# Regrouping the routed slots, shortening the store lag and moving the row weighting to ScalarE in an AdaLN mixture-of-experts block

## The chip, the core and the metric

One core of a Trainium2 chip runs the whole kernel. The metric is the device time of one execution in microseconds; of the kernel before, three runs are known, with a median of 580.17 us (579.09 to 580.22).

## What is computed

The input x holds 32 sequences of 256 rows of 128 float32 values: 8192 rows. Per sequence, six vectors come from a small product (`mod = silu(c) @ wmod`). Then:

```
h = layernorm(x) * (1 + ca) + sa
x = x + ga * attention(h)          # linear attention, 32 memory channels
h = layernorm(x) * (1 + cb) + sb
gate = softmax(h @ w_gate.T); the two best of 8 experts per row, with their scores
x = x + gb * sum over the two of  score * (gelu(h @ W1[e] + b1[e]) @ W2[e] + b2[e])
```

The hidden width of an expert is 512. Only the two chosen experts of a row are computed.

## The kernel before, in words

**Attention steps.** Two sequences make a pair (4 tiles of 128 rows), 16 pairs in all. A software pipeline of steps (`steps`, L231) runs on PE, DVE and ACT; step p handles the projections of pair p, the attention product of pair p-1 and the second norm and the logits of pair p-2. Steps -1 to 3 and 14 to 17 are written out, the ones between run in loops of two steps each. Eight steps also turn one piece of the expert weights into float16 high and low parts (`weights_high` L519 on ACT, `weights_low` L736 on DVE), and SP moves each piece back (`move`, L365), behind the load of a memory matrix and the clearing of a part of the slot buffer (L382 to L388).

**Routing.** The pairs form three groups (`GPAIRS`, L23). After a group's pairs, `route` (PE L1100, ACT L617, DVE L827) picks two experts per row and gives each row two places (`POS`) in a DRAM buffer of slots: a slot is 256 rows of one expert. A group of n tiles has n + 7 slots (`ST`, L33), so the three groups have 31, 31 and 23, in all 85. POOL then scatters the rows with indirect DMAs (`scatter`, L473), two per tile: 128 DMAs in all.

**Slots.** After all steps a loop of 85 slots runs in ten turns of 8 and a rest (`ffn_loop`, L249). For slot t PE does `up(t)` and then `down(t-2)` (L1112, L1123), ACT the Gelu of t (L627), DVE the high and low split of t-1 and the result rows of t-3 (L942, L951). SP's queue (`ring`, L357) alternates: the load of slot t, which waits until `up(t-4)` is done, and then the store of slot t - LAG, which waits for that slot's rows. LAG is 8.

**Gathering and mixing.** The results return to the rows in 16 chunks of 4 tiles. POOL's queue holds first all scatters; then for each group it waits until all slots of the group are stored and gathers the group's chunks, 8 indirect DMAs per chunk (`gather`, L483, the DMA is L490), and after each chunk's DMAs it waits for the chunk before and flags it (`landed`, L494, the memset L497). The ring has 8 places, so the gather of chunk c waits until chunk c-8 is mixed. DVE mixes a chunk in four passes (`mix`, L960): both results by their scores (L967), their sum (L971), by the gate (L976), onto x (L979). Chunks 0 to 3 are mixed in turns 6 to 9 of the slot loop, one pass after every second slot (`MIX0`, L49, is 31 // 8 + 3 = 6), chunks 4 to 15 after the loop (L983). SP writes a mixed chunk out (L411), 16 in all, after all stores.

Of the kernel before, what the change touches and what calls it, by code (L numbers as in the profile page):

```python
# [6 lines left out]
def build_adaln_block(nc, A):  # L7
    f32, f16 = mybir.dt.float32, mybir.dt.float16
    i32, u32 = mybir.dt.int32, mybir.dt.uint32
    ALU, ACT, AX = mybir.AluOpType, mybir.ActivationFunctionType, mybir.AxisListType  # L10
    ds = bass.ds

    BATCH, SEQ, D = 32, 256, 128
# [4 lines left out]
    PAIRS = BATCH // 2  # L18
# [1 line left out]
    W = D + 1  # L20
    LN_EPS, CLIP = 1e-5, 1e-6

    GPAIRS = (6, 6, 4)  # L23
    GROUPS = len(GPAIRS)
    PAIRS_TO = [sum(GPAIRS[:g + 1]) for g in range(GROUPS)]
    GT = tuple(n * PT for n in GPAIRS)
# [6 lines left out]
    ST = tuple(2 * TOK * n // SLOT + E - 1 for n in GT)  # L33
    S0 = tuple(sum(ST[:g]) for g in range(GROUPS + 1))
    SLOTS = S0[-1]
    LAG = 2 * RING
    BODY = 2 * RING
    TURNS = SLOTS // BODY
    JT = 2 * TOK * GTM // 2 // SLOT
# [6 lines left out]
    LOOPED = 4  # L46
    ZS = 8
    ZERO0 = tuple(sum(-(-s // ZS) for s in ST[:g]) for g in range(GROUPS + 1))
    MIX0 = S0[1] // BODY + 3  # L49
    KB = FF // 128  # L50

    ctx = ExitStack()
    with ctx:
# [6 lines left out]
        def sem(name):  # L60
            return ctx.enter_context(nc.semaphore(name))
# [145 lines left out]
        y_out = [sem(f"y_out{k}") for k in range(RING)]  # L207
        up_done, g_ready = sem("up_done"), sem("g_ready")
        ghigh_ready, glow_ready, down_done, y_ready = sem("ghigh_ready"), sem("glow_ready"), sem("down_done"), sem("y_ready")
        gathered = [sem(f"gathered{n}") for n in range(2)]  # L210
        rows_in, mix_link, mixed, out_done = sem("rows_in"), sem("mix_link"), sem("mixed"), sem("out_done")

        block = ctx.enter_context(nc.Block())
# [1 line left out]
        def ge(eng, s, v):  # L215

            if isinstance(v, int) and v <= 0:
                return
            eng.wait_ge(s, v)
# [11 lines left out]
        def steps(eng, step, route, after={}, weights=False, last=lambda: None):  # L231


            for p in range(-1, 4):
                step(p, p % 2, p // 2)
                after.get(p, lambda: None)()

            for first, end, n_of, g in ((0, 2, 0, 0), (2, 4, 1, None), (4, 5, None, 1)):
                with eng.Fori(first, end) as n:
                    for k in range(2):  # L240
                        step(2 * n + 4 + k, k, n + 2, **({"weights": n_of} if weights and n_of is not None else {}))
                if g is not None:
                    route(g)
            for p in range(PAIRS - 2, PAIRS + 2):
                step(p, p % 2, p // 2)
            last()
            route(GROUPS - 1)

# [61 lines left out]
        def _(sp):  # L310
# [46 lines left out]
            def ring(n, g=None, h=None):  # L357

                for k in range(RING):
                    if not isinstance(n, int) or RING * n + k < SLOTS:  # L360
                        load(g, n, k)
                    if not isinstance(n, int) or LAG <= RING * n + k < SLOTS + LAG:
                        store(h, n - LAG // RING, k)

            def move(c):  # L365

# [15 lines left out]
            for p in range(LOOPED, PAIRS):  # L382
                sp.wait_ge(fold_ready, p - EARLY + 1)
                if p > LOOPED + 1:
                    sp.wait_ge(mem_done, p - 1)
                sp.dma_start(MR[:, p % 2, :], MEMO[:, p, :]).then_inc(mr_in[p % 2], 16)
                clear(p - LOOPED)
                move(2 * (p - LOOPED - 1))  # L388

            for i in range(2):  # L390
                sp.wait_ge(ws_moved[i], 16 * (E + 1))
# [2 lines left out]
            sp.dma_start(GA[:].rearrange("p (b d) -> p b d", d=D),  # L394
                         gsc[:, D:2 * D].rearrange("(o b) d -> o b d", o=1).broadcast_to([128, BATCH, D])).then_inc(gb_in, 16)
            ring(1)
            n = LAG // RING
            cuts = sorted(S0[1:] + tuple(s + LAG for s in S0[1:-1]))
            for cut in cuts:
                if cut // RING - n > 1:  # L400
# [112 lines left out]
        def _(act):  # L513
# [28 lines left out]
            def step(p, j, half, weights=None):  # L542
                q, r = p - 1, p - 2
                if has(r):

                    ge(act, var_ready, r + 1)
                    nc.scalar.activation(rstd2[:, 1, :], rstd2[:, 0, :], ACT.Ln).then_inc(ln2_ln, 1)
                    ge(act, ln2_ln, r + 1)
                    nc.scalar.activation(rstd2[:, 2, :], rstd2[:, 1, :], ACT.Exp, scale=-0.5).then_inc(ln2_exp, 1)
                if has(p - 3):  # L550
                    rows(p - 3)
                if has(p):

                    ge(act, qk_done, p + 1)
                    ge(act, sig_ready, p)
                    nc.scalar.activation(RL[:], psQK[:, 0:SEQ], ACT.Relu, scale=-1.0).then_inc(rl_link, 1)
                    ge(act, rl_link, p + 1)
                    nc.scalar.activation(EX[:], RL[:], ACT.Exp, scale=-1.0).then_inc(er_ready, 1)
                if has(q):

                    ge(act, am_ready, q + 1)
                    nc.scalar.activation(AM[:, :, TOK:SEQ], psS.rearrange("p (b c) -> p b c", b=2)[:, :, TOK:SEQ],
                                         ACT.Copy).then_inc(am_side, 1)
                if has(r):

                    ge(act, xn2_turned, r + 1)
                    ge(act, lo_ready, r)
                    if isinstance(r, int) and r == 0:
                        act.wait_ge(bnd_all, 2)
                    for b in range(2):  # L570
                        last = nc.scalar.activation(  # L571
                            H2T[:, b * SEQ:(b + 1) * SEQ], psH[:, b * SEQ:(b + 1) * SEQ], ACT.Identity,
                            bias=modT[:, ds(3 * BATCH + 2 * r + b, 1)], scale=modT[:, ds(4 * BATCH + 2 * r + b, 1)])
                    last.then_inc(h2t_ready, 1)
                    ge(act, h2t_ready, r + 1)
                    ge(act, parts_turned, r)
                    nc.scalar.activation(HH[:], H2T[:], ACT.Copy).then_inc(hi_ready, 1)  # L577
                if has(p + 1):

                    if isinstance(p, int) and p + 1 in NORMS:  # L580
                        act.wait_ge(ln1_ready, NORMS.index(p + 1) + 1)
                    ge(act, xn_turned, p)
                    for t in range(PT):
                        last = nc.scalar.activation(XN[:, 1 - j, t * D:(t + 1) * D], X[:, ds((p + 1) * PT * D + t * D, D)],  # L584
                                                    ACT.Identity, bias=shift1[:, ds((p + 1) * PT + t, 1)],
                                                    scale=rstd1[:, ds((p + 1) * PT + t, 1)])
                    last.then_inc(xn_ready, 1)
                if has(p):

                    ge(act, sig_ready, p + 1)  # L590
                    for b in range(2):
                        last = nc.scalar.activation(KT[b * 64:b * 64 + DM, j, :], SIG[b * 64 + DM:b * 64 + 64, j, :],
                                                    ACT.Copy)
                    last.then_inc(kt_ready, 1)
                if weights is not None:
                    act.wait_ge(ws_ready, 4)
                    weights_high(2 * half - 4 + j, weights)
                if has(p):
                    ge(act, v_done, p + 1)
                    ge(act, av_done, p - 1)  # L600
                    if isinstance(p, int) and p == 0:
                        act.wait_ge(const_ready, 4)
                    nc.scalar.activation(VP[:, j, :, 1:W], psV[:].rearrange("p (t d) -> p t d", d=D),
                                         ACT.Copy).then_inc(vp_ready, 1)
                if has(p + 1):

                    if isinstance(p, int) and p == -1:
                        act.wait_ge(mod_ready, 1)
                    ge(act, xn_turned, p + 2)
                    ge(act, v_done, p)  # L610
                    for b in range(2):
                        last = nc.scalar.activation(
                            HT[:, 1 - j, b * SEQ:(b + 1) * SEQ], psX[:, b * SEQ:(b + 1) * SEQ], ACT.Identity,
                            bias=modT[:, ds(2 * (p + 1) + b, 1)], scale=modT[:, ds(BATCH + 2 * (p + 1) + b, 1)])
                    last.then_inc(hT_ready, 1)
# [20 lines left out]

            act.wait_ge(pos_ready, 1)
            ffn_loop(act, ((0, gelu, True),))

        TOP, TINY = 2.0 ** 14, 2.0 ** -40  # L640

# [5 lines left out]
        def _(dve):  # L647
# [96 lines left out]
            def step(p, j, half, weights=None):  # L744
# [75 lines left out]
                    nc.vector.tensor_scalar(LGT[:, ds(r * PT * E, PT * E)], psQK[:, SEQ:SEQ + PT * E], x_scales[:, 4:5], None,  # L820
                                            ALU.mult).then_inc(lgt_ready, 1)
                if weights is not None:
                    weights_low(4 * half - 8 + 2 * j, weights)

            route_link = links(dve, route_step, 0)

# [130 lines left out]
                nc.vector.scalar_tensor_tensor(out=halves(YR[:, k, :]), in0=halves(psD[k % 2][:, 0:SH * D]),  # L957
                                               scalar=f_scales[:, 4:5], in1=bias, op0=ALU.mult, op1=ALU.add).then_inc(y_ready, 1)

            def mix(c, place, part):  # L960

                y = YG[:, ds(place * 2 * CH * D, 2 * CH * D)].rearrange("p (k t d) -> p k t d", k=2, t=CH)
                if part == 0:
# [2 lines left out]
                    cw = CW[:, :, ds(c * CH, CH)].rearrange("p k (t o) -> p k t o", o=1).broadcast_to([128, 2, CH, D])  # L966
                    nc.vector.tensor_tensor(y, y, cw, ALU.mult).then_inc(mix_link, 1)  # L967
                    return
                ge(dve, mix_link, 3 * c + part)
                if part == 1:  # L970
                    nc.vector.tensor_tensor(y[:, 0], y[:, 0], y[:, 1], ALU.add).then_inc(mix_link, 1)  # L971
                elif part == 2:
# [7 lines left out]

            dve.wait_ge(pos_ready, GROUPS)
            ffn_loop(dve, ((-1, split, False), (-3, rows, True)), mix)
            for first, last in ((TURNS - MIX0, YRING), (YRING, CHUNKS)):  # L983
                with dve.Fori(first, last) as c:
                    for part in range(4):
                        mix(c, c - first // YRING * YRING, part)

        @block.tensor
        def _(pe):
# [181 lines left out]
```

## Time and profile before

| | us |
|---|---|
| median of 3 runs | 580.17 |
| the profiled execution's own time | 579.69 |
| its span | 578.0 |
| DVE busy | 464.3 (80%) |
| PE busy | 379.8 (66%) |
| POOL busy | 314.8 (54%) |
| ACT busy | 305.3 (53%) |

The page gives, of one profiled execution, the busy time of each engine, the span in 40 slices of 14.45 us, and the chain of work that ended last. The timeline gives single instructions: its first number is the start in us from the start of the span, its second the duration in us. "SPq" is SP's queue of DMA issues. A busy time of POOL at an indirect DMA is the time in which it prepares the transfer, not the transfer.

### The profile page before, as it was taken

Reading aid. Unit: us, or ns where it says so; the run is one execution under the profiler, and the core shown is the slowest. Engines: PE = TensorE matmul, PEld = TensorE weight load, DVE = VectorE, ACT = ScalarE, POOL = GpSimd, SP = SyncE. Lnnn points to the kernel's source line nnn. Section 1 sums busy time; section 2 is a strip of 40 time slices with the busy share of each in tenths; the row PEclk is TensorE's granted clock in tenths of the full one; section 3 lists DMA queues with packets and bytes.
Section 4 is the critical chain, followed back from the end, with each engine's and each line's share of the span. In section 5 each row is a group of like instructions: output and inputs, shape, how many; then the busy total and the mean of one; then the engine's idle time right before and its main releaser. Section 6 shows DMA issues by size and latency. Waiting matters only on the chain.

```text
span 578.0 us, 14761 instructions
## 1 busy us (share of the span) xinstructions
PE 379.8 (66%) x4184; PEld 337.1 (58%) x4185; DVE 464.3 (80%) x1092; ACT 305.3 (53%) x658; POOL 314.8 (54%) x344
## 2 busy tenths in 40 slices
PE   3550557761877718428999999999999999700000
PEld 3350546650766617317989999998989889600000
DVE  4669888888888898666888888899999999786424
ACT  1441557981898817417667776677666666400000
POOL 3258100001777727777777200778860887788672
PEclk9955777875788958758999999999999999955555
DMA  3499002543558522513755443556553555453231
GB/s 107 146 344 341 2 1 65 154 140 92 157 164 237 168 51 87 166 50 91 143 142 145 109 100 93 143 141 136 139 127 93 131 132 138 114 161 112 64 86 54
DMA packets 129664, 73.19 MB, mean 127 GB/s; under 512 B 53728, under 2 KB 122976, under 8 KB 129376
## 3 DMA queue, kind: packets, MB, share of 16 engines
q1 hardware_dynamic: 121440, 56.02, 35.0%
q0 software_dynamic: 8192, 16.79, 11.0%
q8 instruction: 14, 0.23, 0.2%
q14 instruction: 18, 0.15, 0.1%
HBM read 21.75 MB, written 34.90 MB: 98 GB/s over the span
## 4 chain that ended last, share of the span: by engine, by line
PE 38%; DVE 26%; POOL 16%; issue 10%; ACT 4%; DMA 3%; DVEq 2%; SPq 0%; ACTq 0%; POOLq 0%
PE psA L1131 16%; POOL ROW L490 16%; PE psA L1119 8%; PE psV L1119 4%; PE psH L1119 4%; DVE ATT L734 3%; PE psH L1029 2%; DVE X L803 2%; DMA X<-in_x 2%; DVE stats L677 2%; DVE stats L810 2%; DVE w_bound L913 2%; ACT HH L577 1%; ACT ATT L571 1%; DVE HL L796 1%
## 5 line engine op out<-in xcount | busy, mean ns | idle before, releaser
L490 POOL DMA_INDIRECT ROW<-slot_out,POS x128 | 150.0, 1172 | 93.5 <-DMA slot_out<-VP 54.6
L479 POOL DMA_INDIRECT slot_rows<-ROW,POS x128 | 131.5, 1027 | 115.1 <-DVE EXPT L888 76.7
L1131 PE MATMUL psA<-WST,ATT 128*128 x2040 | 139.0, 221 | 2.1 <-DVE VP L957 1.6
L1131 PEld LDWEIGHTS psA<-WST,ATT 128*128 128x128 f16 x2040 | 124.9, 98 | 12.4 <-issue 3.7
L948 DVE SCALAR_TENSOR_TENSOR ATT<-ATT,f_scales 128x1024 f16<-128x1024 f32 x85 | 109.2, 1284 | 3.0
L632 ACT ACTIVATE ATT<-psA,b1T,f_scales 128x256 f32<-128x256 f32 x172 | 83.1, 564 | 35.7 <-PE psA L1119 35.7
L946 DVE TENSOR_SCALAR ATT<-ATT,f_scales 128x1024 f16<-128x1024 f32 x85 | 65.3, 768 | 21.9 <-ACT ATT L632 21.2
L1119 PE MATMUL psA<-WT,WST 128*128 128x256 f16 x516 | 65.7, 279 | 5.7 <-DVE RT L876 3.7
L632 ACT ACTIVATE ATT<-psV,b1T,f_scales 128x256 f32<-128x256 f32 x84 | 42.9, 561 | 36.9 <-PE psH L1119 35.2
L1119 PEld LDWEIGHTS psA<-WT,WST 128*128 x516 | 48.5, 99 | 13.5 <-issue 6.2
L1029 PE MATMUL psH<-ident,ATT 128*128 128x128 f32 x64 | 14.2, 360 | 57.1 <-DVE ATT L734 57.1
L1029 PEld LDWEIGHTS psH<-ident,ATT 128*128 128x128 f32 x64 | 9.1, 178 | 64.9 <-DVE ATT L734 64.9
L632 ACT ACTIVATE ATT<-psH,b1T,f_scales 128x256 f32<-128x256 f32 x84 | 42.9, 567 | 0.0
L957 DVE SCALAR_TENSOR_TENSOR VP<-psA,f_scales,b2B 128x256 f32<-128x256 f32 x85 | 40.5, 478 | 1.9 <-PE psA L1131 1.9
L967 DVE TENSOR_TENSOR ROW<-ROW,CW x16 | 19.6, 1223 | 25.4 <-POOL flag L497 25.3
L1119 PE MATMUL psV<-WT,WST 128*128 128x256 f16 x252 | 34.7, 275 | 0.0
L1119 PE MATMUL psH<-WT,WST 128*128 128x256 f16 x252 | 34.4, 273 | 0.0
L571 ACT ACTIVATE ATT<-psH,modT 128x256 f32<-128x256 f32 x32 | 16.3, 560 | 27.9 <-PE psH L1029 27.9
L584 ACT ACTIVATE ATT<-X,shift,rstd 128x128 f32<-128x128 f32 (+1 forms) x64 | 26.2, 479 | 0.9 <-DVE shift L687 0.9
L1119 PEld LDWEIGHTS psH<-WT,WST 128*128 x252 | 24.7, 98 | 2.9
L796 DVE TENSOR_TENSOR HL<-ATT,HH 128x512 f16<-128x512 f32 x16 | 11.1, 693 | 17.4 <-ACT HH L577 17.4
L1049 PE MATMUL psV<-GA,ATT 128*128 128x128 f32 (+1 forms) x128 | 25.0, 361 | 0.0
(199 smaller groups left out, 696.4 us busy)
## 6 DMA issues: line engine op xcount, KB each, us to landing
slot_out<-VP SPq DMA_DIRECT2D x85, 128.0 KB
slot_rows<-zero SPq DMA_DIRECT2D x8, 1024.0 KB, 7.2
X<-in_x SPq DMA_DIRECT2D x8, 512.0 KB, 7.4
WST<-in_W SPq DMA_DIRECT2D x2, 2048.0 KB, 11.8
WST<-WT SPq DMA_DIRECT2D x16, 256.0 KB, 2.3
out<-X SPq DMA_DIRECT2D x16, 256.0 KB, 2.4
slot_rows<-zero SPq DMA_DIRECT2D x3, 896.0 KB, 4.8
slot_rows<-ROW,POS POOLq DMA_INDIRECT x128
```

Source lines behind the costliest of these rows:

```text
L479: nc.gpsimd.indirect_dma_start(xg[g], bass.IndirectOffsetOnAxis(ap=POS[:, k * TILES + t:k * TILES + t + 1], axis=0), ROW[:, t * 2 * D:(t + ...
L490: nc.gpsimd.indirect_dma_start(YG[:, o:o + D], None, yg[g], bass.IndirectOffsetOnAxis(ap=POS[:, i:i + 1], axis=0)).then_inc(gathered[c % 2 ...
L571: last = nc.scalar.activation(H2T[:, b * SEQ:(b + 1) * SEQ], psH[:, b * SEQ:(b + 1) * SEQ], ACT.Identity, bias=modT[:, ds(3 * BATCH + 2 * ...
L584: last = nc.scalar.activation(XN[:, 1 - j, t * D:(t + 1) * D], X[:, ds((p + 1) * PT * D + t * D, D)], ACT.Identity, bias=shift1[:, ds((p + ...
L632: last = nc.scalar.activation(G[:, k % 2, m * SLOT:(m + 1) * SLOT], psU[k % 2][m // 2][:, m % 2 * SLOT:(m % 2 + 1) * SLOT], ACT.Gelu, bias ...
L946: nc.vector.tensor_scalar(GH[:, k % 2, :], G[:, k % 2, :], f_scales[:, 3:4], None, ALU.mult).then_inc(ghigh_ready, 1)
L948: nc.vector.scalar_tensor_tensor(out=GL[:, k % 2, :], in0=G[:, k % 2, :], scalar=f_scales[:, 3:4], in1=GH[:, k % 2, :], op0=ALU.mult, op1= ...
L957: nc.vector.scalar_tensor_tensor(out=halves(YR[:, k, :]), in0=halves(psD[k % 2][:, 0:SH * D]), scalar=f_scales[:, 4:5], in1=bias, op0=ALU. ...
L1029: last = nc.tensor.transpose(psH[:, t * D:(t + 1) * D], XN2[:, t * D:(t + 1) * D], ident[:])
L1049: last = mm(psV[:, t * D:(t + 1) * D], HT[:, j, t * TOK:(t + 1) * TOK], GA[:, ds((2 * p + t // 2) * D, D)], start=True, stop=True)
L1119: last = mm(o, W1S[:, ds(e * 2 * FF + a * FF + m * 128, 128)], XT[:, k, b * SLOT:(b + 1) * SLOT], start=(c == 0), stop=(c == 2))
L1131: last = mm(psD[k % 2][:, h * D:(h + 1) * D], a[:, k % 2, i:i + TOK], W2S[:, ds(e * 2 * FF + b * FF + m * D, D)], start=(m == 0 and c == 0 ...
```

## The change

Four things. The groups become 7, 5 and 4 pairs: 28, 20 and 16 tiles, with 35, 27 and 23 slots, still 85; `steps` and SP's moves are rearranged to it (the eight weight pieces go to steps 5 to 12 instead of 4 to 11; the first routing follows step 8 instead of 7, the second follows step 13 as before). LAG becomes 6. `MIX0` is written with + 2; 35 // 8 + 2 is 6. After its last Gelu, ACT multiplies the gathered rows of chunks 4 to 14 by their scores, one instruction of 128x128 for each of 8 tiles, and DVE does three passes for these chunks instead of four; chunk 15 keeps four passes on DVE.

```diff
-    GPAIRS = (6, 6, 4)
+    GPAIRS = (7, 5, 4)
...
-    LAG = 2 * RING
+    LAG = 6
...
-    MIX0 = S0[1] // BODY + 3
+    MIX0 = S0[1] // BODY + 2
+    MIXED = TURNS - MIX0
...
-            for p in range(-1, 4):
+            for p in range(-1, 5):
                 step(p, p % 2, p // 2)
                 after.get(p, lambda: None)()
 
-            for first, end, n_of, g in ((0, 2, 0, 0), (2, 4, 1, None), (4, 5, None, 1)):
+            for g, (first, end) in enumerate(((2, 4), (4, 6))):
                 with eng.Fori(first, end) as n:
                     for k in range(2):
-                        step(2 * n + 4 + k, k, n + 2, **({"weights": n_of} if weights and n_of is not None else {}))
-                if g is not None:
+                        step(2 * n + 1 + k, 1 - k, n + k, **({"weights": (g, 2 * n - 4 + k)} if weights else {}))
+                if g == 0:
                     route(g)
-            for p in range(PAIRS - 2, PAIRS + 2):
+            for p in range(PAIRS - 3, PAIRS + 2):
                 step(p, p % 2, p // 2)
+                if p == PAIRS_TO[1] + 1:
+                    route(1)
...
-                        store(h, n - LAG // RING, k)
+                        store(h, n + (k - LAG) // RING, (k - LAG) % RING)
...
-                move(2 * (p - LOOPED - 1))
+                move(2 * (p - LOOPED - 2))
...
             ffn_loop(act, ((0, gelu, True),))
+
+            act.wait_ge(pos_ready, GROUPS)
+            for first, last in ((MIXED, YRING), (YRING, CHUNKS - 1)):
+                with act.Fori(first, last) as c:
+                    ge(act, rows_in, c + 1)
+                    for k in range(2):
+                        for t in range(CH):
+                            y = YG[:, ds((c - first // YRING * YRING) * 2 * CH * D + (k * CH + t) * D, D)]
+                            done = nc.scalar.activation(y, y, ACT.Copy, scale=CW[:, k, ds(c * CH + t, 1)])
+                    done.then_inc(scaled, 1)
...
-                ge(dve, mix_link, 3 * c + part)
+                if part == 1 and by_act:
+                    ge(dve, scaled, c - MIXED + 1)
+                else:
+                    ge(dve, mix_link, (3 * c if base is None else base) + part)
...
-            for first, last in ((TURNS - MIX0, YRING), (YRING, CHUNKS)):
+            for first, last in ((MIXED, YRING), (YRING, CHUNKS - 1)):
                 with dve.Fori(first, last) as c:
-                    for part in range(4):
-                        mix(c, c - first // YRING * YRING, part)
+                    for part in range(1, 4):
+                        mix(c, c - first // YRING * YRING, part, 3 * MIXED + 2 * (c - MIXED) - 1, True)
+            for part in range(4):
+                mix(CHUNKS - 1, CHUNKS - 1 - YRING, part, 3 * MIXED + 2 * (CHUNKS - 1 - MIXED))
```

## Rows read from the trace of the kernel before

**Rows 1.** The page, part 2: busy tenths of PE and POOL in 40 slices
```profile
PE   3550557761877718428999999999999999700000
...
POOL 3258100001777727777777200778860887788672
```

**Rows 2.** The page, part 4: the chain that ended last, by line
```profile
PE psA L1131 16%; POOL ROW L490 16%; PE psA L1119 8%; PE psV L1119 4%; PE psH L1119 4%; DVE ATT L734 3%; PE psH L1029 2%; DVE X L803 2%; DMA X<-in_x 2%; DVE stats L677 2%; DVE stats L810 2%; DVE w_bound L913 2%; ACT HH L577 1%; ACT ATT L571 1%; DVE HL L796 1%
```

**Rows 3.** Timeline of POOL: start us, us, line, out<-in, count, idle before and releaser
```profile
142.00 1.31 POOL L479 DMA_INDIRECT slot_rows<-ROW,POS  x1 [66.33 <-DVE EXPT L888]
...
359.98 0.99 POOL L490 DMA_INDIRECT ROW<-slot_out,POS  x1 [37.74 <-DMA slot_out<-VP]
...
429.95 0.09 POOL L497 MEMSET flag<- 1x1 f32 x1
446.92 2.09 POOL L490 DMA_INDIRECT ROW<-slot_out,POS  x1 [16.88 <-DMA slot_out<-VP]
...
506.17 0.09 POOL L497 MEMSET flag<- 1x1 f32 x1
...
510.30 1.44 POOL L490 DMA_INDIRECT ROW<-slot_out,POS  x1 [0.30 <-issue]
512.04 1.77 POOL L490 DMA_INDIRECT ROW<-slot_out,POS  x1 [0.30 <-issue]
...
521.71 1.42 POOL L490 DMA_INDIRECT ROW<-slot_out,POS  x1 [0.22 <-issue]
...
534.79 0.95 POOL L490 DMA_INDIRECT ROW<-slot_out,POS  x1 [0.21 <-issue]
...
567.09 0.09 POOL L497 MEMSET flag<- 1x1 f32 x1
```

**Rows 4.** Timeline of SP's queue in the slots
```profile
357.00 0.58 SPq L355 DMA_DIRECT2D slot_out<-VP  x1
...
361.43 1.20 SPq L347 DMA_TRANSPOSE WT<-slot_rows  x1
...
437.37 1.19 SPq L347 DMA_TRANSPOSE WT<-slot_rows  x1
...
440.02 1.19 SPq L347 DMA_TRANSPOSE WT<-slot_rows  x1
...
444.12 0.58 SPq L355 DMA_DIRECT2D slot_out<-VP  x1
```

**Rows 5.** Timeline of DVE at slot 61's rows and at the last slot's
```profile
438.47 0.48 DVE L957 SCALAR_TENSOR_TENSOR VP<-psA,f_scales,b2B 128x256 f32<-128x256 f32 x1
...
503.61 0.48 DVE L957 SCALAR_TENSOR_TENSOR VP<-psA,f_scales,b2B 128x256 f32<-128x256 f32 x1 [1.89 <-PE psA L1131]
```

**Rows 6.** Timeline of DVE after the slots: passes of the first chunk and the last
```profile
504.13 1.23 DVE L967 TENSOR_TENSOR ROW<-ROW,CW  x1
505.50 0.69 DVE L971 TENSOR_TENSOR ROW<-ROW  x1
...
507.24 0.69 DVE L979 TENSOR_TENSOR X<-X,ROW  x1
...
574.35 0.69 DVE L979 TENSOR_TENSOR X<-X,ROW  x1
```

**Rows 7.** Timeline of ACT in one attention step and at the last slot
```profile
167.34 1.64 ACT L584 ACTIVATE ATT<-X,shift,rstd 128x128 f32 x4
...
496.90 1.93 ACT L632 ACTIVATE ATT<-psA,b1T,f_scales 128x256 f32<-128x256 f32 x4 [0.73 <-PE psA L1119]
```

**Rows 8.** Timeline of SP's queue in the attention steps
```profile
117.15 1.13 SPq L370 DMA_DIRECT2D WST<-WT  x2
...
127.90 1.13 SPq L370 DMA_DIRECT2D WST<-WT  x2
...
205.07 5.68 SPq L347 DMA_TRANSPOSE WT<-slot_rows  x4
```

**Rows 9.** Timeline of PE at the first slot
```profile
257.82 2.74 PE L1119 MATMUL psA<-WT,WST 128*128 128x256 f16 x12 [3.71 <-DVE RT L876]
```

More of the change, by code:

```diff
@@ L209, in build_adaln_block @@
         ghigh_ready, glow_ready, down_done, y_ready = sem("ghigh_ready"), sem("glow_ready"), sem("down_done"), sem("y_ready")
-        gathered = [sem(f"gathered{n}") for n in range(2)]
+        gathered, scaled = [sem(f"gathered{n}") for n in range(2)], sem("scaled")
         rows_in, mix_link, mixed, out_done = sem("rows_in"), sem("mix_link"), sem("mixed"), sem("out_done")
@@ L396, in _ @@
             ring(1)
-            n = LAG // RING
+            n = 2
             cuts = sorted(S0[1:] + tuple(s + LAG for s in S0[1:-1]))
@@ L596, in step @@
                     act.wait_ge(ws_ready, 4)
-                    weights_high(2 * half - 4 + j, weights)
+                    weights_high(weights[1], weights[0])
                 if has(p):
@@ L822, in step @@
                 if weights is not None:
-                    weights_low(4 * half - 8 + 2 * j, weights)
+                    weights_low(2 * weights[1], weights[0])
             route_link = links(dve, route_step, 0)
@@ L958, in rows, with mix @@
                                                scalar=f_scales[:, 4:5], in1=bias, op0=ALU.mult, op1=ALU.add).then_inc(y_ready, 1)
-            def mix(c, place, part):
+            def mix(c, place, part, base=None, by_act=False):
                 y = YG[:, ds(place * 2 * CH * D, 2 * CH * D)].rearrange("p (k t d) -> p k t d", k=2, t=CH)
```

## The prediction, made blind

> **What bounds the kernel now.** First the slices of the page, then the chain, then POOL's timeline. The slices [rows 1] show three stretches: attention, the slots at nine tenths of PE from slice 18 to slice 34, and an end in which PE does nothing and POOL works. The chain that ended last [rows 2] gives 16% of the span, 92 us, to the gathers of L490. That is more than the end after the slots (503.6 to 578), so the chain leaves PE while the slots still run. POOL's timeline [rows 3] shows where. Its gathers of group 0 run from 359.98 to 429.95: 48 in 70.0 us. It then sits idle for 16.9 us until slot 61's store has landed, and from 446.92 it never again waits for another engine: chunks 6 to 10 until the flag at 506.17, chunk 11 until 521.71, chunks 12 to 15 until the flag at 567.09. The last slot's rows are finished at 503.61 + 0.48 = 504.09 [rows 5]. So group 2's gathers could start at about 507 and start at 521.71, because POOL is one chunk behind. The end is set by POOL's backlog, and behind it by two mixes and the last write.
>
> **Regrouping: one chunk leaves the stretch after slot 61.** Group 1 now has 5 chunks instead of 6; the slots, scatters and gathers keep their number. Where does group 0's seventh chunk go? Group 0 is stored with slot 34 instead of 30. Slot 30's store is issued at 357.00 [rows 4] and the gather follows at 359.98 [rows 3], 2.98 later. With LAG 6 the store of slot 34 stands behind the load of slot 40, which is two loads after load 38 and starts at 361.43 [rows 4]; 1.2 for the load's own issue gives 362.6, and the first gather at 365.6, 5.6 later than now. Its first 48 gathers then end at about 429.95 + 5.6 = 435.6, and eight more at 1.33 (70.0 us / 48 is 1.46, with longer gathers in it that come once a turn; I take 10.9 for this chunk) end at 446.5. That is the moment at which group 1 starts today (446.92), so POOL's 16.9 us of idle time take up the chunk. Chunks 7 to 11 then take what chunks 6 to 10 take now, 506.17 - 446.92 = 59.3, and POOL is free at 506.
>
> **LAG 6.** Slot 61's store is issued at 444.12, behind load 69; it now follows load 67 of 437.37 and the rows of slot 61, ready at 438.47 + 0.48 = 438.95 [rows 4, 5]. It is 5.2 earlier, lands at about 441, and is off the path, as POOL is still on group 0. What counts is slot 34's store: at LAG 8 it would be 5.5 later and the whole chain of gathers with it. Behind the waiting store stands the next load, 68: it can't go before 440.02 today, since it waits for PE [rows 4], and the store's issue of 0.4 to 0.6 from 438.95 is over by then. So no load moves. The cover is half a microsecond wide, and a rival below is about it. At the end of the slots nothing changes, since no load stands before the last stores.
>
> **Steps, routing and scatters.** The number of steps, of steps with weights (8), of clears (12 instead of 11, one piece more but the same order of bytes) and of routings stays. SP's order of memory load, clear and move is only shifted by one step, as are the pieces it waits for, so no memory load stands behind another wait than before. The first routing comes one step later, 127.90 - 117.15 = 10.75 [rows 8], so POOL's scatters start at 142.00 + 10.75 = 152.8 instead of 142.00 [rows 3]. The first 56 at 1.27 end at 224, and slot 0's loads, now at 205.07 [rows 8], come at about 226, still 32 us ahead of PE's first slot at 257.82, which waits for the last routing [rows 9]. All scatters end at 322 now (359.98 - 37.74, rows 3), at most 10.75 later then, and still before 365.6. The wider routing tiles (28 tiles instead of 24 in the first, 20 in the second) cancel. I put all of this at 0; for what the trace can't show (a step that meets scatters at another moment) I bound it by 1 us either way. MIX0 remains 6, so this edit does nothing; its first rows are flagged about 5.6 later, at 387, and used from turn 6 on, at 399, so DVE doesn't wait.
>
> **The gathers of group 2.** Their start is the later of POOL (506), the last store and chunk 4's mix. The last store can be issued at 504.1; from slot 61's store to the gather it took 446.92 - 444.12 = 2.8 [rows 3, 4], which makes 507.0. ACT ends its last Gelu at 496.90 + 1.93 = 498.8 [rows 7] and needs, by the four 128x128 instructions in 1.64 [rows 7], 0.41 each, 8 x 0.41 = 3.3 per chunk, 3.4 with the loop. Chunk 4 is weighted at 502.3, DVE's three passes take 507.93 - 505.50 = 2.4 [rows 6] and end at 506.6. So 507.0, where it is 521.71 now: 14.7 gained.
>
> How fast are they? While DVE mixes without a break, two gathers with their gaps take 1.44 + 0.30 + 1.77 + 0.30 = 3.8, 1.9 each [rows 3]. Once DVE waits, 24 gathers take 567.09 - 534.79 = 32.3, 1.35 each. In the rows the long gathers end together with one of DVE's passes of 0.69. After the change the seven chunks 4 to 10, which have been gathered, come to DVE every 3.4 us from ACT, and chunk 11 follows: DVE mixes until about 529. In such a period a gather that is held to the end of a pass fits twice: 1.7 each, against bounds of 1.35 (no hold) and 1.9 (as now). I take 1.7: 13 gathers until 529.1. The other 19 at 1.35 take 25.6, and the last flag but one comes at 554.7 instead of 567.09: 12.4 gained of the 14.7.
>
> The Trainium skill (SBUF — State Buffer, Who interferes with whom) would have it otherwise: a VectorE tensor_tensor with two inputs in SBUF contends with GpSimd's reads, and, as it infers, not with the writing of descriptors. By it all 32 gathers would go at 1.35. The trace of before does not agree: they go at 1.9 beside these passes [rows 3, 6].
>
> **The end.** Today, from the flag at 567.09: 0.36, four passes for chunk 14, four for chunk 15 (3.8 each), and from 574.35 + 0.69 = 575.04 to 578.0 the last write, 10.9 in all [rows 3, 6]. Now ACT's 3.4 and three passes (2.5) stand for chunk 14's 3.8: 2.1 more, 13.0. DVE can't use the wait for chunk 15, since it stands behind it in its queue. The span ends at 554.7 + 13.0 = 567.7, 10.3 less. The weighting instruction is not in the trace; L584 has its shape and engine and is my lower bound. The upper one is the Gelu of 128x256 at 1.93 / 4 = 0.48 [rows 7]: then this end is 0.6 longer, and the stretch of mixing 8 x 0.56 = 4.5 longer, with 2.6 gathers more at 1.7 instead of 1.35, 0.9: 1.5 us in all, which the range holds.
>
> **The sum.** 579.69 - 10.3 = 569.4 on the profiled execution, which lies 0.5 under the median; against the median it is 569.9. I say 569.7.
>
> **Rivals.**
> (a) The gathers of group 2 run undisturbed, since DVE has gaps (also what the page's rule gives by itself): 32 x 1.35 = 43.2 from 507.0, flag at 550.2, end at 563.2, time 565. For it speak the fast gathers beside single chunks; against it the locked pairs of today. Chance 0.17.
> (b) POOL arrives late or stays slow: its spare time before 507.0 is one microsecond by my sum, so a first gather two slots later (5.5), slower gathers in the slots, or ACT at 0.48 give 572 to 576 (569.7 + 5.5 = 575.2 for the first). Chance 0.18.
> (c) Slower: the store's wait holds up the loads. Place: SP's queue, load t+7 behind store t. Today load 68 leaves half a microsecond for it; in turns with a mix pass DVE's rows can be later by that pass (0.69). If PE then waited for its input in each of 79 slots, 10.3 / 79 = 0.13 us per slot would eat the gain, and 0.5 us per slot would give 579.7 - 10.3 + 40 = 609. Against it: the input of a slot is loaded three slots ahead, 8 us. Chance 0.04.
> (d) No change: the backlog isn't what counts, as the gathers are limited by their transfers and the group's total of 128 is the same. Against it: POOL's busy time with its fixed gaps of 0.30 fills that stretch. Chance 0.03.
>
> The forecast itself, 567 to 572, has 0.58. The range leaves out the far side of (b), (c) and (d): 564.5 to 574.5. About 0.2% (1.2 us) can be told from no change here: faster 0.93, same 0.03, slower 0.04.
>
> **What would show it.** Gathers in one run without a wait for stores between group 0 and group 1; the first gather near 365.6; a gap of at most a few us before group 2, whose first gather starts near 507; gathers of 1.7 with gaps until about 529; ACT at 3.4 per chunk; 13 us from the last flag but one to the end; PE's slots ending at 503.5 as now. Wrong it would be if PE's slots ended later (rival c), if group 2 started after 510 (rival b), or if the end after the flag were over 15 us.

## The result and the profile after

The changed kernel takes 571.18 us (median of four runs, 571.0 to 572.52), the kernel before 580.19 in the same comparison. The ratio is 0.9841, 95% interval 0.9822 to 0.9860: 9.0 us less by the medians, 9.2 by the ratio. Forecast were 569.7 us, with a range of 564.5 to 574.5. The profiled execution after is the longest of the four: it took 572.52, with a span of 570.8.

The first view is again the page, its busy slices and its chain by line. L493 is the gather, L1137 and L1149 are the slots' matmuls.

```profile
PE   3551646874377646626999999999999999930000
...
POOL 2248200000277777777777500077878878788671
...
PE psA L1149 16%; POOL ROW L493 14%; PE psA L1137 8%; PE psV L1137 4%; PE psH L1137 4%; DVE ATT L747 3%; PE psH L1047 3%; DVE X L816 2%; DMA X<-in_x 2%; DVE stats L690 2%; DVE stats L823 2%; DVE w_bound L926 2%; ACT HH L580 1%; ACT ATT L574 1%; DVE AM L778 1%
```

Against [rows 1], POOL's empty slices lie together between scatters and gathers, and the dents (2 among the scatters, 0 among the gathers) are gone. The gathers' share of the chain fell from 16% to 14% [rows 2]. POOL's timeline shows the same in single rows:

```profile
371.50 1.06 POOL L493 DMA_INDIRECT ROW<-slot_out,POS  x1 [47.87 <-DMA slot_out<-VP]
...
454.18 1.35 POOL L493 DMA_INDIRECT ROW<-slot_out,POS  x1 [0.30 <-issue]
455.52 0.09 POOL L500 MEMSET flag<- 1x1 f32 x1
455.83 1.02 POOL L493 DMA_INDIRECT ROW<-slot_out,POS  x1 [0.23 <-DMA slot_out<-VP]
...
513.17 0.09 POOL L500 MEMSET flag<- 1x1 f32 x1
513.48 1.44 POOL L493 DMA_INDIRECT ROW<-slot_out,POS  x1 [0.22 <-issue]
515.23 1.23 POOL L493 DMA_INDIRECT ROW<-slot_out,POS  x1 [0.30 <-issue]
516.76 1.13 POOL L493 DMA_INDIRECT ROW<-slot_out,POS  x1 [0.30 <-issue]
518.19 1.46 POOL L493 DMA_INDIRECT ROW<-slot_out,POS  x1 [0.30 <-issue]
...
536.39 0.94 POOL L493 DMA_INDIRECT ROW<-slot_out,POS  x1 [0.21 <-issue]
539.49 1.14 POOL L493 DMA_INDIRECT ROW<-slot_out,POS  x1 [2.16 <-issue]
...
559.05 0.09 POOL L500 MEMSET flag<- 1x1 f32 x1
```

What to see: between group 0 (from 371.50) and group 1 (from 455.83) there is no idle time, where 16.88 us stood in [rows 3]. But neither is there any before group 2, which starts at 513.48. The last slot's rows are done at 506.44 + 0.48 = 506.92, so POOL is still 3.7 us behind what the stores would allow (506.92 + 2.9, the time from a store to the gather that waited for it). The queue, not the last store, still sets the end.

SP's queue at slot 34 and DVE's and ACT's timelines after the slots:

```profile
366.47 1.19 SPq L350 DMA_TRANSPOSE WT<-slot_rows  x1
368.71 0.37 SPq L358 DMA_DIRECT2D slot_out<-VP  x1
369.12 1.19 SPq L350 DMA_TRANSPOSE WT<-slot_rows  x1
```

```profile
368.20 0.48 DVE L970 SCALAR_TENSOR_TENSOR VP<-psA,f_scales,b2B 128x256 f32<-128x256 f32 x1
...
506.44 0.48 DVE L970 SCALAR_TENSOR_TENSOR VP<-psA,f_scales,b2B 128x256 f32<-128x256 f32 x1 [1.89 <-PE psA L1149]
506.89 0.69 DVE L987 TENSOR_TENSOR ROW<-ROW  x1
507.81 0.69 DVE L992 TENSOR_TENSOR ROW<-ROW,GA  x1 [0.23 <-DVE ROW L987]
508.65 0.69 DVE L995 TENSOR_TENSOR X<-X,ROW  x1
509.30 0.69 DVE L987 TENSOR_TENSOR ROW<-ROW  x1
...
522.87 0.69 DVE L995 TENSOR_TENSOR X<-X,ROW  x1
528.66 0.69 DVE L987 TENSOR_TENSOR ROW<-ROW  x1 [5.10 <-ACT ROW L650]
...
562.09 0.69 DVE L987 TENSOR_TENSOR ROW<-ROW  x1 [8.01 <-ACT ROW L650]
```

```profile
501.54 16.46 ACT L650 ACTIVATE ROW<-ROW,CW  x56
...
559.38 2.44 ACT L650 ACTIVATE ROW<-ROW,CW  x8 [8.01 <-POOL flag L500]
```

In the order of the views: slot 34's store (368.71) leaves 0.03 us after its rows (368.20 + 0.48), and the next load goes right behind it. ACT weighs seven chunks in 16.46, so 2.4 each, and DVE takes a chunk every 2.4 (506.89 to 509.30).

The stretches of two executions can be compared only from a common mark, since the attention part varies (shown below). The table gives, from the first slot's first matmul on: the first gather, the first gather of group 2, the last flag but one, and the end of the span. The marks come from one profile of each kernel, the times are medians; the kernel before was measured anew beside each set of runs (580.2 to 581.2), and the ratio is to that.

| kernel | first gather | group 2 | flag | end | time | ratio to before (95%) |
|---|---|---|---|---|---|---|
| before | 102.2 | 263.9 | 309.3 | 320.2 | 580.2 | 1 |
| changed | 111.3 | 253.2 | 298.8 | 310.6 | 571.2 | 0.9841 (0.9822-0.9860) |
| LAG 8 | 113.5 | 254.8 | 299.9 | 311.7 | 572.8 | 0.9869 (0.9840-0.9897) |
| LAG 7 | 110.7 | 252.6 | 298.2 | 309.9 | 571.4 | 0.9848 (0.9825-0.9872) |
| groups 6, 6, 4 | 99.6 | 257.2 | 301.8 | 313.5 | 574.8 | 0.9892 (0.9855-0.9928) |
| four passes on DVE | 111.0 | 254.4 | 304.0 | 314.9 | 575.6 | 0.9923 (0.9894-0.9952) |
| fewer gathers | 111.1 | 249.5 | 293.6 | 305.3 | 565.9 | 0.9749 (0.9727-0.9771) |
| ACT to chunk 13 | 111.0 | 252.9 | 298.5 | 308.3 | 569.8 | 0.9819 (0.9799-0.9839) |
| before, ACT alone | 101.7 | 260.3 | 303.9 | 315.5 | 576.4 | 0.9929 (0.9902-0.9955) |
| before, LAG 6 alone | 99.8 | 260.0 | 306.5 | 317.4 | 578.8 | 0.9958 (0.9941-0.9975) |

### The profile page after: what moved, and what is told of

It is laid out like the page before. It is cut to its first block, busy times and chain, and to the rows that moved or that the text cites. A ratio compares the mean times of both kernels' runs of the same rounds, so it can differ in the third digit from the quotient of the medians.

```text
span 570.8 us, 14921 instructions
## 1 busy us (share of the span) xinstructions
PE 382.1 (67%) x4184; PEld 339.5 (59%) x4185; DVE 450.4 (79%) x1081; ACT 331.5 (58%) x746; POOL 312.9 (55%) x344
## 3 DMA queue, kind: packets, MB, share of 16 engines
q0 software_dynamic: 8192, 16.79, 11.1%
## 4 chain that ended last, share of the span: by engine, by line
PE 39%; DVE 27%; POOL 14%; issue 10%; ACT 4%; DMA 3%; DVEq 2%; ACTq 0%; SPq 0%
PE psA L1149 16%; POOL ROW L493 14%; PE psA L1137 8%; PE psV L1137 4%; PE psH L1137 4%; DVE ATT L747 3%; PE psH L1047 3%; DVE X L816 2%; DMA X<-in_x 2%; DVE stats L690 2%; DVE stats L823 2%; DVE w_bound L926 2%; ACT HH L580 1%; ACT ATT L574 1%; DVE AM L778 1%
## 5 line engine op out<-in xcount | busy, mean ns | idle before, releaser
L493 POOL DMA_INDIRECT ROW<-slot_out,POS x128 | 147.0, 1148 | 86.6 <-DMA slot_out<-VP 48.1
L1149 PE MATMUL psA<-WST,ATT 128*128 x2040 | 139.1, 221 | 2.0 <-DVE VP L970 1.6
L1149 PEld LDWEIGHTS psA<-WST,ATT 128*128 128x128 f16 x2040 | 125.0, 98 | 12.3 <-issue 3.6
L1137 PE MATMUL psA<-WT,WST 128*128 128x256 f16 x516 | 65.7, 279 | 5.9 <-DVE RT L889 3.7
L1137 PEld LDWEIGHTS psA<-WT,WST 128*128 x516 | 48.4, 99 | 13.9 <-issue 6.6
L650 ACT ACTIVATE ROW<-ROW,CW x88 | 26.2, 395 | 34.0 <-POOL flag L500 34.0
L987 DVE TENSOR_TENSOR ROW<-ROW (+1 forms) x16 | 11.0, 689 | 31.2 <-ACT ROW L650 31.2
L1137 PE MATMUL psV<-WT,WST 128*128 128x256 f16 x252 | 34.8, 275 | 0.0
L1137 PE MATMUL psH<-WT,WST 128*128 128x256 f16 x252 | 34.4, 273 | 0.0
L574 ACT ACTIVATE ATT<-psH,modT 128x256 f32<-128x256 f32 x32 | 16.3, 560 | 28.7 <-PE psH L1047 28.7
L1137 PEld LDWEIGHTS psH<-WT,WST 128*128 x252 | 24.7, 98 | 2.9
L809 DVE TENSOR_TENSOR HL<-ATT,HH 128x512 f16<-128x512 f32 x16 | 11.1, 693 | 18.4 <-ACT HH L580 18.4
```

Of the source, the lines that this page charges most:

```text
L493: nc.gpsimd.indirect_dma_start(YG[:, o:o + D], None, yg[g], bass.IndirectOffsetOnAxis(ap=POS[:, i:i + 1], axis=0)).then_inc(gathered[c % 2 ...
L574: last = nc.scalar.activation(H2T[:, b * SEQ:(b + 1) * SEQ], psH[:, b * SEQ:(b + 1) * SEQ], ACT.Identity, bias=modT[:, ds(3 * BATCH + 2 * ...
L650: done = nc.scalar.activation(y, y, ACT.Copy, scale=CW[:, k, ds(c * CH + t, 1)])
L1137: last = mm(o, W1S[:, ds(e * 2 * FF + a * FF + m * 128, 128)], XT[:, k, b * SLOT:(b + 1) * SLOT], start=(c == 0), stop=(c == 2))
L1149: last = mm(psD[k % 2][:, h * D:(h + 1) * D], a[:, k % 2, i:i + TOK], W2S[:, ds(e * 2 * FF + b * FF + m * D, D)], start=(m == 0 and c == 0 ...
```

## The experiments

**The kernel before, a second profile.** No edit.

> The kernel before, unchanged, for a second profile. In the first profiles the first slot's matmuls start at 257.8 us before and at 260.2 us after the change. Theory A: the change itself costs the attention part 2 us; then this run starts its slots at 257.5 to 258.1. Rival B: the start varies from execution to execution by 1 to 3 us whatever the kernel; then it starts somewhere between 257 and 261, and the slots that follow take 245.8 us as before (from the first matmul to the last slot's rows).

```profile
261.75 2.74 PE L1119 MATMUL psA<-WT,WST 128*128 128x256 f16 x12 [3.71 <-DVE RT L876]
```

The same program starts its slots 3.9 us later than in [rows 9], and took 582.89. From the mark on its span is 319.4 (320.2 before). A falls, and B holds, with a start somewhat beyond its 261: the 2.4 us by which the changed kernel's profile starts its slots later (260.24) are no effect of the change that these profiles could tell. Over all profiles here the first slot starts at 257.4 to 261.7 (median 259.8) in the ten with the changed steps, and at 257.8 to 261.8 (median 259.5) in the four with those of before.

**LAG 8.**

```diff
-    LAG = 6
+    LAG = 2 * RING
```

> The changed kernel with LAG back at 8. Theory A: the gathers form one run from slot 34's store to the end, so every us of that store counts, but at LAG 8 it left SP only 2.2 us after the rows were ready, and at LAG 6 it leaves at once: first gather, first gather of group 2 and the end all 2.2 us later, time 573.4. Rival B (my blind sum): a store two loads earlier is 5.5 us earlier, so LAG 8 costs 5.5: 576.7. Rival C: the last slot's store sets group 2, and the lag costs nothing: 571.2.

572.76 us. First gather 2.2 later, as A has it; of that 1.6 reach group 2 and 1.1 the end. The intervals of the two ratios overlap, so the size rests on the profiles. DVE's rows of slot 34 and SP's queue show why it is not 5.5:

```profile
367.66 0.48 DVE L970 SCALAR_TENSOR_TENSOR VP<-psA,f_scales,b2B 128x256 f32<-128x256 f32 x1
...
369.07 1.19 SPq L350 DMA_TRANSPOSE WT<-slot_rows  x1
370.31 0.58 SPq L358 DMA_DIRECT2D slot_out<-VP  x1
372.03 1.19 SPq L350 DMA_TRANSPOSE WT<-slot_rows  x1
```

At LAG 8 slot 34's store (370.31) goes 1.24 behind the start of its load, and that load starts 0.9 after the rows (367.66 + 0.48).

**Groups of 6, 6 and 4.**

```diff
-    GPAIRS = (7, 5, 4)
+    GPAIRS = (6, 6, 4)
...
-    MIX0 = S0[1] // BODY + 2
+    MIX0 = S0[1] // BODY + 3
...
-                pe.wait_ge(vp_ready, min(PAIRS, PAIRS_TO[g] + 2))
-                pe.wait_ge(row_ready, PAIRS_TO[g])
+                pe.wait_ge(vp_ready, (9, 14, 16)[g])
+                pe.wait_ge(row_ready, (7, 12, 16)[g])
```

> The changed kernel with groups of 6, 6 and 4 pairs again, its steps, lag and ScalarE weighting kept. Theory A: six chunks follow slot 61's store instead of five behind an unbroken queue; first gather of group 1 at about 447, of group 2 at about 520.5 instead of 513.5, some of it given back since fewer gathers meet the mixing: time about 576.5. Rival B (my blind sum): the regrouping is worth a whole chunk and the last store sets group 2's start, 13 us: 584, slower than before the change. Rival C: POOL isn't the limit, 571.2.

574.79 us, 3.6 above the changed kernel, and 2.9 from the mark to the end. Its ratio's interval just touches that of the changed kernel, and the marks agree. The mechanism is A's, its size smaller: 4.0 of A's 7 us at group 2, 3.6 of 5.3 in the time. POOL again waits 16.3 us for slot 61; but the first gather comes 11.7 us earlier (99.6 against 111.3), so the regrouping is worth 16.3 - 11.7 = 4.6 at most, and 4.0 arrive at group 2.

**Four passes on DVE.** ACT's loop is taken out, and DVE's last loops are those of the kernel before.

```diff
-            act.wait_ge(pos_ready, GROUPS)
-            for first, last in ((MIXED, YRING), (YRING, CHUNKS - 1)):
...
-            for first, last in ((MIXED, YRING), (YRING, CHUNKS - 1)):
+            for first, last in ((MIXED, YRING), (YRING, CHUNKS)):
                 with dve.Fori(first, last) as c:
-                    for part in range(1, 4):
-                        mix(c, c - first // YRING * YRING, part, 3 * MIXED + 2 * (c - MIXED) - 1, True)
-            for part in range(4):
-                mix(CHUNKS - 1, CHUNKS - 1 - YRING, part, 3 * MIXED + 2 * (CHUNKS - 1 - MIXED))
+                    for part in range(4):
+                        mix(c, c - first // YRING * YRING, part)
```

> The changed kernel with all four passes of chunks 4 to 15 on VectorE again. Theory A: VectorE's unbroken passes hold up POOL's gathers; seven chunks in 26.7 us let 14 gathers through at 1.9 us each, where three passes per chunk let 19 through in the same time, which costs 5 x 1.28 = 6.4 us; the end after the last flag but one is 0.9 us shorter (10.9 instead of 11.75): time 576.7. Rival B (tensor_tensor passes don't hold up the gathers' descriptors): only the end changes, 570.3. Rival C: the weighting moves nothing but the end, and the gathers' rate of the first chunks is set by the stores' and outputs' traffic: 570.3 with gathers of 1.5 us as now.

575.57 us, 4.4 more, where A said 5.5. POOL's timeline at group 2's first gathers, to be set beside the same rows of the changed kernel above:

```profile
513.35 1.76 POOL L493 DMA_INDIRECT ROW<-slot_out,POS  x1 [0.23 <-issue]
515.42 1.44 POOL L493 DMA_INDIRECT ROW<-slot_out,POS  x1 [0.30 <-issue]
517.16 1.76 POOL L493 DMA_INDIRECT ROW<-slot_out,POS  x1 [0.31 <-issue]
519.23 1.44 POOL L493 DMA_INDIRECT ROW<-slot_out,POS  x1 [0.30 <-issue]
```

Pairs of 3.8 are back, where three gathers take 513.48 to 518.19 = 4.7 in the changed kernel: 1.9 against 1.57. The 32 gathers of group 2 take 49.7 instead of 45.6, chunk 11 before them meets the same (group 2 starts 1.1 later), and the end is 0.9 shorter. B and C fall. The page of the Trainium skill that infers that tensor_tensor passes leave the writing of descriptors alone (SBUF — State Buffer, Who interferes with whom) does not agree with this pair of runs, as far as it is meant for indirect DMAs: what differs there is one VectorE pass in four, done by ScalarE instead, and the gathers beside the passes take 1.9 or 1.57. But the same section of the Trainium skill also states that such passes contend with GpSimd instructions that read SBUF, and each of these gathers takes its row numbers (`POS`) from there. The runs don't show which of the two holds them up.

**Fewer gathers.** Chunks 0 to 11 gather 6 of their 8 pieces; the output lacks two tiles of the second expert's results in each.

```diff
-                    for t in range(CH):
+                    for t in range(CH if k == 0 or c >= 12 else CH - 2):
...
-                pool.wait_ge(gathered[c % 2], 16 * 2 * CH * (c // 2 + 1))
+                pool.wait_ge(gathered[c % 2], 16 * (6 * min(c // 2 + 1, 6) + 8 * max(c // 2 - 5, 0)))
```

> The changed kernel, in which chunks 0 to 11 gather only 6 of their 8 pieces (two tiles of the second expert's results are left out of the output), so that POOL reaches group 2 some 34 us before the last slot is stored. Theory A: then the last store sets group 2's start, 2.9 us after the last slot's rows, 3.6 us earlier than now against the first slot; about three more gathers meet the mixing and give 0.8 back: time 568.4. Rival B: POOL's queue isn't what holds group 2 back: 571.2. The slots themselves keep their 246 us under either.

565.91 us, 5.3 less, where A said 2.8. POOL's timeline, and in it the last store and the end of chunk 4's mix:

```profile
485.15 1.21 POOL L493 DMA_INDIRECT ROW<-slot_out,POS  x1 [4.14 <-DVE X L995]
...
493.01 0.65 POOL L500 MEMSET flag<- 1x1 f32 x1
...
503.75 0.37 SPq L358 DMA_DIRECT2D slot_out<-VP  x1
505.44 0.69 DVE L995 TENSOR_TENSOR X<-X,ROW  x1
...
506.93 0.94 POOL L493 DMA_INDIRECT ROW<-slot_out,POS  x1 [13.27 <-DVE X L995]
...
540.85 0.94 POOL L493 DMA_INDIRECT ROW<-slot_out,POS  x1 [0.21 <-issue]
542.09 0.94 POOL L493 DMA_INDIRECT ROW<-slot_out,POS  x1 [0.30 <-issue]
...
551.01 0.09 POOL L500 MEMSET flag<- 1x1 f32 x1
```

Group 2 starts at 506.93 - 257.42 = 249.5 from the mark, 3.7 earlier: A holds for the start, and the floor is reached. The row names chunk 4's mix as what came last (DVE's L995 at 505.44 + 0.69 = 506.13), but that was done 0.8 us before. Chunk 11's first gather (485.15), which waited for such a pass, came 0.3 after it (484.20 + 0.68 = 484.88). The last store was issued 3.2 before the gather, about what other stores took to their gathers (2.6 to 3.0), so the store is the likelier one; the profile doesn't settle it. The rest is a thing that I had not counted: the pause of 2.16 us after the first gather of chunk 14, in the timeline above, is missing here (540.85, 542.09).

**ScalarE only to chunk 13.**

```diff
-            for first, last in ((MIXED, YRING), (YRING, CHUNKS - 1)):
+            for first, last in ((MIXED, YRING), (YRING, CHUNKS - 2)):
...
-            for part in range(4):
-                mix(CHUNKS - 1, CHUNKS - 1 - YRING, part, 3 * MIXED + 2 * (CHUNKS - 1 - MIXED))
+            for c in (CHUNKS - 2, CHUNKS - 1):
+                base = 3 * MIXED + 2 * (CHUNKS - 2 - MIXED) + 3 * (c - CHUNKS + 2)
+                for part in range(4):
+                    mix(c, c - YRING, part, base)
```

> The changed kernel with chunk 14 weighted by VectorE too (ScalarE does chunks 4 to 13). Theory A: after the last flag but one VectorE's first sum starts 3.0 us later now (ScalarE's 2.44 and its wake-up); with its own pass of 1.23 it starts after 0.4 + 1.4 = 1.8, so the end is 1.2 us earlier: 570.0. Rival B: the last chunk's own landing (1.6 us after that flag) or its store bounds the end: 571.2.

569.84 us, 1.3 less, where A said 1.2; the intervals of the two ratios overlap. DVE and POOL at the end:

```profile
558.29 0.09 POOL L500 MEMSET flag<- 1x1 f32 x1
558.48 1.22 DVE L980 TENSOR_TENSOR ROW<-ROW,CW 128x1024 f32<-128x1024 f32 x1 [5.16 <-POOL flag L500]
559.74 0.69 DVE L987 TENSOR_TENSOR ROW<-ROW 128x512 f32<-128x512 f32 x1
```

The sum of chunk 14 starts 1.45 after the flag, against 562.09 - 559.05 = 3.04 in the changed kernel. These passes are written out, which also takes away the small gaps between them that the loop has.

**ScalarE for chunk 15, VectorE for chunk 14.** As the last one, with ACT's eight instructions for chunk 15 behind its loop and three passes on DVE.

```diff
+            act.wait_ge(rows_in, CHUNKS)
...
+            dve.wait_ge(scaled, CHUNKS - 1 - MIXED)
+            for part in range(1, 4):
+                mix(CHUNKS - 1, CHUNKS - 1 - YRING, part, base + 2)
```

> The changed kernel with VectorE weighting chunk 14 and ScalarE chunk 15. Theory A: after the last flag but one VectorE is through chunk 14 at 0.4 + 3.6 = 4.0 us, ScalarE through weighting chunk 15 at 1.6 + 0.3 + 2.4 = 4.3; then three passes, so the end is 0.9 us shorter than where VectorE weighs both (569.8): 569.0. Rival B: the last write and what is ahead of it in its queue bound the end: 569.8.

569.51 us, ratio 0.9811 (0.9785 to 0.9836), against 0.9819. By the profile the end after the flag is 567.5 - 558.16 = 9.3 instead of 9.8; the times can't tell the two kernels apart. Both lie below the changed kernel, but all three intervals overlap; that either beats it rests on the end measured in the profiles (9.8 and 9.3 us instead of 11.75) and on medians 1.3 and 1.7 lower, and is not shown beyond that.

**LAG 7.**

```diff
-    LAG = 6
+    LAG = 7
```

> The changed kernel with LAG 7. Theory A: the store of slot t stands behind load t+7, which goes when the matmuls of slot t+3 are done, just before the rows of slot t are; so it leaves with the rows as at LAG 6: 571.2, first gather 111.3 us after the first slot's matmul. Rival B: each slot of lag costs the same, half of what LAG 8 costs: 572.0 and 112.4.

571.35 us, first gather at 110.7 from the mark: A, with 0.6 that no theory named and that is within what profiles differ by.

**ACT's weighting alone, on the kernel before.** The same edits as in the change to ACT and to `mix`, with groups 6, 6, 4 and LAG 8.

```diff
             ffn_loop(act, ((0, gelu, True),))
+            act.wait_ge(pos_ready, GROUPS)
+            for first, last in ((MIXED, YRING), (YRING, CHUNKS - 1)):
...
```

> The kernel before with the ScalarE weighting alone (groups 6, 6, 4 and LAG 8 kept). Theory A: group 2's gathers start 4 us earlier, as the last chunk before them no longer meets unbroken four-pass mixing, the first of them go 1.6 us faster, and the end after the last flag but one is 0.9 us longer: 580.3 - 4.7 = 575.6. Rival B: passes on VectorE don't hold the gathers: 581.1.

576.42 us, 4.4 less than before (580.77 in that comparison). Group 2 starts 3.6 earlier, the flag comes 5.4 earlier, the end 4.7: A.

**LAG 6 alone, on the kernel before.**

```diff
-    LAG = 2 * RING
+    LAG = 6
...
-                        store(h, n - LAG // RING, k)
+                        store(h, n + (k - LAG) // RING, (k - LAG) % RING)
...
-            n = LAG // RING
+            n = 2
```

> The kernel before with LAG 6 alone. Theory A: slot 61's store leaves 2.1 us earlier, with the rows, and the six chunks and the end follow: 580.3 - 2.1 = 578.2. Rival B: it leaves 5.2 us earlier, as I worked out blind: 575.1.

578.82 us (581.23 before in that comparison), ratio 0.9958 (0.9941 to 0.9975): 2.4 less. A; the 5.2 of B lie outside the interval.

**LAG 5 and LAG 4.** The same line of the changed kernel with 5 and 4.

> The changed kernel with LAG 5. The load of slot t+6 then stands behind the store of slot t and leaves with that slot's rows, 4.9 us before its matmuls (at LAG 6 it is 7.8). Theory A: a load takes less than that, nothing moves: 571.2. Rival C (mine, blind: the waiting store holds up the loads): a load takes about 6 us, PE loses 1.1 us in each of 80 slots: 660.

> The changed kernel with LAG 4: the load of slot t+5 leaves 2.0 us before its matmuls are due. Theory A: a load takes 3 to 4 us (its issue alone 1.2), so PE waits 1 to 2 us in each of 80 slots: 650 to 730 us. Rival B: the load is there in 2 us: 571.2.

LAG 5: 572.89 us, ratio 0.9874 (0.9845 to 0.9903). By the profile the slots, from the mark to the last slot's rows, take 247.3 instead of 246.7. By the spans theory A holds but for half a us (311.2 from the mark to the end, 310.6 in the changed kernel); the median is 1.7 higher, with overlapping intervals, which these profiles don't explain. LAG 4: one execution, 616.13 us, below A's 650 and far above B's 571.2. The waits of PE for its slot's input (us in all, times, longest):

```profile
PE psA L1137 <- DMA WT<-slot_rows: 11.2, 14, 2.2
PE psV L1137 <- DMA WT<-slot_rows: 10.6, 12, 1.7
```

Of the other runs only LAG 5 has such a wait, one of 0.2 us. The slots take 553.36 - 260.15 = 293.2. These two rows add up to 21.8 us, and in the chain that ended last these loads stand with 9% of the span, 55 us, where the changed kernel's chain shows none. So the mechanism of my rival (c) exists: it costs next to nothing at LAG 5 and much at LAG 4. At LAG 4 it costs 46.5 / 85 = 0.55 us per slot, less than the 1 to 2 that I gave for it before the run.

## Why the prediction was right, and where its steps were not

The side, the size and the range were right, and the size in part by luck: group 2's start was put 4.0 us too early, its gathers and the end together were priced 3.4 too high, and the two made up for each other.

**What bounds the kernel: right.** The end is the end of POOL's queue. Taking a quarter of 96 gathers away moved the start of group 2 by 3.7 us and no more, as the stores allow, and the time by 5.3, of which the missing pause is a part.

**The regrouping: right; its number carries the error of the lag.** I had the idle 16.9 us minus a start 5.6 later, 11.3. Measured from the mark, the start came 9.1 later (102.2 to 111.3), all of it behind an unbroken queue, so 7.8 of the idle time were won. The 3.5 between are those of the next step: at LAG 8 the start comes 11.3 later (113.5), where my figures give 5.6 + 5.5 = 11.1. With the lag kept, the same regrouping costs 11.7 at the start and brings 16.3: 4.0 at group 2, 3.6 us of time.

**LAG 6: the step that failed.** "The store of slot 34 stands behind the load of slot 40 ... this gives 362.6" looked at the load alone. Slot 34's rows were not ready until 365.4 + 0.48 = 365.9 in the trace of before. And for slot 61 I took the row pass at 438.47, which is slot 60's; slot 61's is at 441.52, so its store at 444.12 was only 2.1 late, not 5.2. The two rows, from the trace of before:

```profile
365.40 0.48 DVE L957 SCALAR_TENSOR_TENSOR VP<-psA,f_scales,b2B 128x256 f32<-128x256 f32 x1
...
441.52 0.48 DVE L957 SCALAR_TENSOR_TENSOR VP<-psA,f_scales,b2B 128x256 f32<-128x256 f32 x1
```

So LAG 6 gives 2.2 us at the store, and 1.6 to 2.4 in the time, by undoing it and by doing it alone. Had this been right, POOL would have come to group 2 as in the sum, at the moment of the last store. In fact it came 6.5 us later than forecast, of which 2.4 are the later start of the slots in this execution, 3.5 this step, and the rest, 0.6, the pace of the 96 gathers: they took 142.0 (371.50 to 513.48) where I had 140.4, less the 1.0 of spare time that I had behind them. By the prediction's own sign, a start of group 2 after 510, this step was wrong.

**Steps and scatters at 0: nothing against it.** The second profile of before shows that an execution varies here by 3.9 us, more than my bound of 1; the medians of the starts, 259.8 and 259.5, differ by 0.3. Smaller effects stay open.

**The gathers beside the mixing: right in kind.** Held gathers, freed in part: 1.57 each, where I took 1.7 between 1.35 and 1.9. They started later, so fewer of them met the unbroken mixing, which itself ended at 522.87 + 0.69 = 523.6 and not at 529: chunk 11, which I had close behind, was gathered later and mixed by itself from 528.66. The seven chunks before it went faster than I had them, by ACT's instruction: 2.44 for eight, 0.31 each, under the 0.41 that I had called a lower bound. L584 takes its bias and scale from vectors, the new one a scale alone; that this makes the difference isn't tested. DVE, not ACT, set the pace. The 32 gathers took 45.6 instead of my 47.7. The weighting as a whole is worth 4.4 us, by undoing it and by doing it alone, the largest of the parts by these medians.

**The end: right in kind.** 11.75 instead of 13.0, again by ACT's shorter instruction; 10.9 before.

**The sum.** From the mark, group 2 starts 10.7 earlier (14.7 forecast), its gathers take 0.2 longer (2.3 forecast), the end 0.85 longer (2.1 forecast): 9.6 in the profiles where 10.3 was forecast, and 9.0 to 9.2 in the times. The parts by single runs, 3.6 (groups), 4.4 (weighting) and 1.6 (lag), add up to 9.6.

**The rivals.** (b) came in by one half: POOL arrived late, but its gathers in group 2 were not slow. (a) did not: beside the unbroken passes no gather went at the undisturbed 1.25. (c) has its place. I wrote that no load moves; that rested on the same wrong row. With LAG 6 alone, load 68 goes at 444.02 - 259.61 = 184.4 from the mark, behind slot 61's store, where it went at 440.02 - 257.82 = 182.2 before. The loads do wait, but they have the time: the slots take 246.7 in the changed kernel against 246.3 before. (d) falls with the fewer gathers: the count of gathers ahead of group 2 does move the end.

## What to carry to other kernels

Where an in-order queue sets the end, time gained in it is worth what is left after the queue's own start: filling an idle gap of 16 us by starting 12 us later brought 4. To find when a waiting store leaves, read both rows, the instruction ahead in its queue and the producer of its data, and count instances from one end of the list, as neighbouring slots look alike. An engine that is idle can be worth using for the sake of a third one: ScalarE's weighting brought 4.4 us because VectorE's passes were holding up POOL.

## What was not expected

POOL pauses for 2.0 to 2.3 us after the first gather of chunk 14 in every kernel that does all gathers, before and after the change (2.16 in the row above). That is after its 241st indirect DMA, 128 scatters and 113 gathers. With 24 gathers left out there are 232 in all, and no pause at that place. What happens at that count, the runs don't show.

ScalarE's multiplication of 128x128 by one scale per row goes at 0.31 us in a run of eight, where the form with scale and bias took 0.41 [rows 7].
